# Attention pieces in DRAM as three rows to a channel, and another order of the work in a step

## The reference

```python
xn = layer_norm(x, norm_w, norm_b)                 # layer 0, 16 heads of 16 channels
q, k = xn @ q_w + q_b, xn @ k_w + k_b
att = softmax(einsum('bnhl,bmhl->bnmh', q, k) + (1 - mask) * -1e6, axis=2)
y = einsum('bnmh,bmhl->bnhl', att, (xn @ v_w + v_b) * mask)
scale, shift = split(silu(emb) @ emb_w + emb_b)
x = x + silu(layer_norm(y, sb_w, sb_b) * (1 + scale) + shift) @ out_w + out_b

xn = layer_norm(x, ln_w, ln_b)                     # layer 1, 8 heads of 32 channels
q = softmax(xn @ Wq + bq, over the head's channels)
k = softmax(xn @ Wk + bk + (1 - mask) * -1e6, over the tokens)
y = q @ (k^T @ ((xn @ Wv + bv) * mask))            # per head
x = x + silu(layer_norm(y) * (1 + scale) + shift) @ W_out + b_out
```

## Time and profile before

| | us |
|---|---|
| median of 3 runs (723.3 to 726.71) | 725.44 |
| the profiled execution | 723.0 |
| its span | 721.2 |
| PE busy in it | 579.2 |
| DVE busy | 441.6 |
| ACT busy | 351.3 |
| POOL busy | 65.9 |

### The profile page before, as it was taken

The page is one execution under the profiler, slowest core; times in us unless marked ns, Lnnn a source line. Parts: engine busy times, 40 slices in busy tenths (PEclk is TensorE's granted clock), DMA queues, the critical chain, the costliest instruction groups (busy, mean ns, idle before and its releaser), DMA issues.

```text
span 721.2 us, 7870 instructions
## 1 busy us (share of the span) xinstructions
PE 579.2 (80%) x2938; PEld 264.8 (37%) x2938; DVE 441.6 (61%) x891; ACT 351.3 (49%) x408; POOL 65.9 (9%) x85
## 2 busy tenths in 40 slices
PE   2608830899989988999998899999897999984875
PEld 1203510323334332434433333445333443333574
DVE  5134540457766896778788588777954788304443
ACT  0310200555556667565666656565545756671431
POOL 1021040000000003010001012000050101000300
PEclk9955855699999997999999799999966999997897
DMA  6143384003341000211102000000000000000001
GB/s 177 53 117 123 119 243 138 21 1 109 108 145 70 18 24 1 69 41 29 47 22 69 12 13 23 1 24 30 24 0 24 30 30 1 2 0 1 0 1 59
DMA packets 19494, 36.40 MB, mean 50 GB/s; under 512 B 3528, under 2 KB 10400, under 8 KB 19424
## 3 DMA queue, kind: packets, MB, share of 16 engines
q1 hardware_dynamic: 19264, 35.85, 16.7%
q10 hardware_dynamic: 192, 0.05, 0.0%
HBM read 20.76 MB, written 14.96 MB: 50 GB/s over the span
## 4 chain that ended last, share of the span: by engine, by line
PE 52%; DVE 17%; DMA 13%; ACT 6%; issue 4%; SPq 4%; ACTq 1%; POOL 0%; POOLq 0%; DVEq 0%
PE bank L849 13%; DMA stack_rows<-late 11%; DVE halfmax L972 10%; PE sT L830 9%; PE bank L738 8%; PE bank L717 8%; SPq L430 3%; PE bank L790 2%; PE sT L717 2%; PE bank L752 2%; DVE stats L903 2%; ACT prob L678 2%; DMA qs<-crows 2%; ACT hT L617 2%; PE bank L759 1%
## 5 line engine op out<-in xcount | busy, mean ns | idle before, releaser
L972 DVE TENSOR_REDUCE halfmax<-bank 128x1 f32<-128x512 f32 x512 | 325.3, 684 | 151.0 <-PE bank L738 149.5
L678 ACT ACTIVATE prob<-sT 128x1024 f32<-128x1024 f32 x256 | 257.4, 1023 | 185.2 <-PE sT L830 184.8
L738 PE MATMUL bank<-ks,qs 50*128 50x512 f32 x512 | 159.1, 455 | 42.7 <-DMA qs<-stack_rows 21.3
L830 PE MATMUL sT<-qs,ks 52*128 52x512 f32 x512 | 132.2, 507 | 45.4 <-DMA qs<-crows 34.5
L849 PE MATMUL bank<-prob,vp 128*17 128x512 f32 x1024 | 143.3, 633 | 4.2 <-ACT prob L678 4.2
L830 PEld LDWEIGHTS sT<-qs,ks 52*128 52x128 f32 x512 | 50.6, 192 | 178.6 <-issue 98.9
L738 PEld LDWEIGHTS bank<-ks,qs 50*128 50x128 f32 x512 | 73.0, 200 | 92.6 <-DVE halfmax L972 63.9
L534 POOL TENSOR_TENSOR rstd<-var,neghalf 128x4 f32<-128x4 f32 x14 | 14.2, 1015 | 591.8 <-DVE var L913 591.8
L717 PE MATMUL bank<-w,hT 128*128 128x256 f32 x144 | 39.1, 409 | 0.5
L849 PEld LDWEIGHTS bank<-prob,vp 128*17 128x17 f32 x1024 | 17.2, 96 | 43.9 <-issue 32.4
L717 PEld LDWEIGHTS bank<-w,hT 128*128 128x128 f32 x144 | 26.8, 202 | 9.0 <-DVE halfmax L972 3.5
(11 more groups left out here) (130 smaller groups left out, 461.0 us busy)
## 6 DMA issues: line engine op xcount, KB each, us to landing
stack_rows<-late SPq DMA_DIRECT2D x32, 256.0 KB
ks<-stack_rows SPq DMA_DIRECT2D x16, 400.0 KB
qs<-stack_rows SPq DMA_DIRECT2D x32, 192.0 KB, 3.4
stack_rows<-late SPq DMA_DIRECT2D x8, 512.0 KB
out_x<-xs SPq DMA_DIRECT2D x4, 512.0 KB, 3.0
xs<-in_x SPq DMA_DIRECT2D x4, 256.0 KB, 3.9
xs<-in_x SPq DMA_DIRECT2D x2, 512.0 KB, 6.5
late<-in_L_cond_emb_w SPq DMA_DIRECT2D x1, 1024.0 KB, 11.2
```

The source lines that it names most:

```text
L678: act.activation(prob[:, c % 2, 2 * u:2 * u + 2, :].rearrange("p j n -> p (j n)"), sT[u][:, :], ACT.Exp).then_inc(exp_done, 1)
L738: last = pe.matmul(o, qs[rows, s % SLOTS, c, t * P:(t + 1) * P], ks[rows, hg, c, half * HALF:(half + 1) * HALF], start=True, stop=True)
L830: last = pe.matmul(sT[u][:, two * HALF:(two + 1) * HALF], ks[rows, hg, u, c * P:(c + 1) * P], qs[rows, s % SLOTS, u, :], start=True, stop= ...
L972: dve.tensor_reduce(halfmax[:, s % 2, r, half:half + 1], o, axis=AX.X, op=ALU.max, negate=True).then_inc(u.done, 1)
```

## The change

It has four parts.

1. `stack_rows` becomes [group, 128 channels, 3 pieces, tokens]. A store writes 64 channels times two pieces, and 64 channels times one piece, for keys and for queries (four transfers instead of five). A load reads "(channel piece)" as 48 rows. The mask no longer goes through `stack_rows`: for batch 0 it is written into all of `ks` once, for batch 1 in two small transfers with every load of keys.
2. The rows of ones are filled from a longer source (1024 elements in `prob` instead of 128 in `ones`), so in fewer pieces. The 17 small loads go from ScalarE's queue to SyncE's, ahead of `store_parts(0)`. Store and keys of group 3, the embedding weights and `load_max(0)` stand in this order ahead of the other weights.
3. A step becomes: maxima 0, scores 0, scores 1, maxima 1, values of the step before, all small work of the step. ScalarE takes both exponentials, then the small work. The vector engine takes maxima 0, a middle part (low parts of "qk", half of the statistics), maxima 1, and the rest.
4. "y" and the layer norms that depend on it come one spot later, and the other items move with them: steps without any small work become 44 (37 before), steps with two items 24 (17).

```diff
         mask_rows = nc.dram_tensor("mask_rows", [B, PARTS, T], F32, kind="Internal").ap()
-        stack_rows = nc.dram_tensor("stack_rows", [G, 2 * GH, ROW_MAX, T], F32, kind="Internal").ap()
+        stack_rows = nc.dram_tensor("stack_rows", [G, P, PIECES, T], F32, kind="Internal").ap()
...
         for s in range(SUBS - 1):
-            at["y", s] = 2 * NT * (s + 1) + 1
+            at["y", s] = 2 * NT * (s + 1) + 2
...
-        spots = [(k, p) for k in range(STEPS + 2) for p in range(2)]
-        pe_at, act_at, dve_at = ({spot: [] for spot in spots} for _ in range(3))
-        begins = {key: (i // 2, i % 2) for key, i in at.items()}
-        for key, spot in begins.items():
-            assert spot[0] < STEPS
-            pe_at[spot].append(key)
+        pe_at, act_at, dve_mid, dve_at = ({k: [] for k in range(STEPS + 2)} for _ in range(4))
+        begins = {key: i // 2 for key, i in sorted(at.items(), key=lambda item: item[1])}
+        for key, k in begins.items():
+            assert k < STEPS
+            pe_at[k].append(key)
             if key[0] == "qk":
-                act_at[spot].append(key)
-                dve_at[later(spot)].append(key)
+                act_at[k].append(key)
+                dve_mid[k + 1].append(key)
             elif key[0] in ON_ACT:
-                act_at[spot].append(key)
+                act_at[k].append(key)
             else:
-                dve_at[spot].append(key)
...
             for i in range(QT):
-                dve_at[k, i // 2].append(("stats", kind, b, h, i))
-            dve_at[k + 1, 0].append(("aggr", kind, b, h))
+                (dve_mid if i < 2 else dve_at)[k].append(("stats", kind, b, h, i))
+            dve_mid[k + 1].append(("aggr", kind, b, h))
...
+        def dve_step(k):
+            if k >= STEPS:
+                return dve_mid[k] + dve_at[k]
+            return maxima(k, 0) + dve_mid[k] + maxima(k, 1) + dve_at[k]
...
-            sp.wait_ge(ones_ready, 1)
-            one = ones[0:PARTS, :].bitcast(F32).unsqueeze(1)
+            sp.wait_ge(one_ready, 1)
+            one = prob[0:PARTS, 0, 0:2, :].rearrange("r j n -> r (j n)").unsqueeze(1)
             for two in range(2):
                 rows = slice(two * TILE + ROW_MASK, two * TILE + ROW_MAX)
-                sp.dma_start(qs[rows, :, :, :].rearrange("r s c (a x) -> r (s c a) x", x=P).bitcast(F32), one.to_broadcast([PARTS, SLOTS * 2 * QT, P])).then_inc(rows_in, 16)
+                sp.dma_start(qs[rows, :, :, :].rearrange("r s c x -> r s (c x)").bitcast(F32), one.to_broadcast([PARTS, SLOTS, T])).then_inc(rows_in, 16)
                 rows = slice(two * TILE + ROW_MAX, two * TILE + ROWS)
-                sp.dma_start(ks[rows, :, :, :].rearrange("r s c (a x) -> r (s c a) x", x=P).bitcast(F32), one.to_broadcast([PARTS, HG * 2 * NT, P])).then_inc(rows_in, 16)
-
+                sp.dma_start(ks[rows, :, :, :].rearrange("r g c x -> r (g c) x").bitcast(F32), one.to_broadcast([PARTS, HG * 2, T])).then_inc(rows_in, 16)
             sp.wait_ge(mask_out, 16 * B)
-            for b in range(B):
-                sp.dma_start(stack_rows[b * HG:(b + 1) * HG, GH:2 * GH, ROW_MASK:ROW_MAX, :].rearrange("g x r n -> g x (r n)"),
-                             mask_rows[b].rearrange("r n -> (r n)").unsqueeze(0).unsqueeze(0).to_broadcast([HG, GH, PARTS * T])).then_inc(fill_in, 16)
+            for two in range(2):
+                rows = slice(two * TILE + ROW_MASK, two * TILE + ROW_MAX)
+                sp.dma_start(ks[rows, :, :, :].rearrange("r g c x -> r (g c) x").bitcast(F32), mask_rows[0].unsqueeze(1).to_broadcast([PARTS, HG * 2, T])).then_inc(rows_in, 16)
+            for at_row in (0, 32):
+                for i, src in enumerate((v_b, bq, bv)):
+                    sp.dma_start(braw[at_row:at_row + 1, i, :], src.rearrange("(o d) -> o d", o=1)).then_inc(braw_in, 16)
+            for name, src, n in (("sb_w", sb_norm_w, KC), ("sb_b", sb_norm_b, KC),
+                                 ("emb_b0", emb_b, 2 * KC), ("ln_w", ln_w, KC), ("ln_b", ln_b, KC), ("bk", bk, KC),
+                                 ("ln2_w", ln2_w, KC), ("ln2_b", ln2_b, KC), ("emb_b1", b_emb, 2 * KC),
+                                 ("cond", cond.rearrange("b e -> (b e)"), B * EC), ("mask1", mask1.rearrange("b t o -> (b t o)"), B * NT)):
+                loads(sp, name, src, n, vecs2, NV0, vec2_in)
 
             def store_parts(g):
 
                 last = unit["qk", g // HG, g % HG, NH - 1]
                 sp.wait_ge(last.done, last.done_at)
-                for xs_of, r, piece in ((slice(0, 2 * GH), 0, 0), (slice(0, GH), 1, 0), (slice(GH, 2 * GH), 2, 0), (slice(0, GH), 2, 1), (slice(GH, 2 * GH), 1, 1)):
-                    sp.dma_start(stack_rows[g, xs_of, r * DH0:(r + 1) * DH0, :], parts[xs_of.start * DH0:xs_of.stop * DH0, g % 2, piece, :]).then_inc(parts_out[g % 2], 16)
+                for side, both, single in ((1, 0, 2), (0, 1, 0)):
+                    rows = slice(side * GC, (side + 1) * GC)
+                    sp.dma_start(stack_rows[g, rows, both:both + 2, :], parts[rows, g % 2, :, :]).then_inc(parts_out[g % 2], 16)
+                    sp.dma_start(stack_rows[g, rows, single, :], parts[rows, g % 2, 0, :]).then_inc(parts_out[g % 2], 16)
 
             def load_keys(g):
                 if g >= HG:
                     sp.wait_ge(sT_ready, 2 * NT * (g + 1))
-                sp.wait_ge(parts_out[g % 2], 16 * 5 * (g // 2 + 1))
+                sp.wait_ge(parts_out[g % 2], 16 * 4 * (g // 2 + 1))
                 for two in range(2):
-                    sp.dma_start(ks[two * TILE:two * TILE + ROW_MAX, g % HG, :, :].bitcast(F32),
-                                 stack_rows[g, GH + 2 * two:GH + 2 * two + 2, :, :].rearrange("c r n -> r c n")).then_inc(k_in[g % HG], 16)
+                    src = stack_rows[g, GC + two * GC // 2:GC + (two + 1) * GC // 2, :, :].rearrange("(c p) r n -> (p r) c n", c=2)
+                    sp.dma_start(ks[two * TILE:two * TILE + ROW_MASK, g % HG, :, :].bitcast(F32), src).then_inc(k_in[g % HG], 16)
+                    if g >= HG:
+                        sp.dma_start(ks[two * TILE + ROW_MASK:two * TILE + ROW_MAX, g % HG, :, :].bitcast(F32),
+                                     mask_rows[g // HG].unsqueeze(1).to_broadcast([PARTS, 2, T])).then_inc(k_in[g % HG], 16)
 
             def load_queries(s):
                 b, n, hg, g = group(s)
                 if s >= SLOTS:
                     sp.wait_ge(sT_ready, 2 * NT * (s - SLOTS + 1))
                 for two in range(2):
-                    sp.dma_start(qs[two * TILE:two * TILE + ROW_MASK, s % SLOTS, :, :].bitcast(F32),
-                                 stack_rows[g, 2 * two:2 * two + 2, 0:ROW_MASK, n * HALF:(n + 1) * HALF].rearrange("c r n -> r c n")).then_inc(q_in[s % SLOTS], 16)
+                    src = stack_rows[g, two * GC // 2:(two + 1) * GC // 2, :, n * HALF:(n + 1) * HALF].rearrange("(c p) r n -> (p r) c n", c=2)
+                    sp.dma_start(qs[two * TILE:two * TILE + ROW_MASK, s % SLOTS, :, :].bitcast(F32), src).then_inc(q_in[s % SLOTS], 16)
...
             store_parts(2)
             load_keys(2)
             load_queries(2)
-            sp.dma_start(wo0[:, :, :], out_w.rearrange("(k p) c -> p k c", p=P)).then_inc(wo_in, 16)
+            store_parts(3)
+            load_keys(3)
+            for i, src in enumerate((emb_w, W_emb)):
+                sp.dma_start(embw[:, i], src.rearrange("(e p) c -> p e c", p=P)).then_inc(embw_in, 16)
+            load_max(0)
             for i, src in enumerate((out_b, b_out)):
                 sp.dma_start(bias_rows[:, i, :], src.partition_broadcast(P)).then_inc(row_in, 16)
-            for i, src in enumerate((emb_w, W_emb)):
-                sp.dma_start(embw[:, i], src.rearrange("(e p) c -> p e c", p=P)).then_inc(embw_in, 16)
-            store_parts(3)
-            load_keys(3)
+            sp.dma_start(wo0[:, :, :], out_w.rearrange("(k p) c -> p k c", p=P)).then_inc(wo_in, 16)
             for i, src in enumerate((Wq, Wk, Wv, W_out)):
                 sp.dma_start(w1[:, i], src.rearrange("(k p) c -> p k c", p=P)).then_inc(w1_in, 16)
...
+            pool.memset(prob[0:PARTS, 0, 0:2, :], 1.0).then_inc(one_ready, 1)
             pool.wait_ge(ident_ready, 1)
+            pool.wait_ge(one_ready, 1)
...
             act.dma_start(m16[:, :], mask0.rearrange("b (t p) -> (b t) p", p=P)).then_inc(m16_in, 16)
-            rows("norm_w", norm_w, KC, True)
-            rows("norm_b", norm_b, KC, True)
+            rows("norm_w", norm_w, KC)
+            rows("norm_b", norm_b, KC)
             for side, src in enumerate((q_b, k_b)):
                 act.dma_start(vecs[COL["qk_b"]:COL["qk_b"] + HG, side * GC:(side + 1) * GC],
                               src.rearrange("(g c) -> g c", c=GC)).then_inc(vec_in, 16)
-            rows("mask0", mask0.rearrange("b t -> (b t)"), B * NT, True)
+            rows("mask0", mask0.rearrange("b t -> (b t)"), B * NT)
             for h in range(NH):
```

(33 more changed lines are left out.)

## The result

The changed kernel takes 674.79 us (median of 4 runs, 673.9 to 676.24) beside 724.37 us of the kernel before on the same chip (4 runs, 720.7 to 726.71): a ratio of 0.932, 95% interval 0.928 to 0.937, or 49.6 us less. 668 us were forecast, with 643 to 690 as the range. Nearly all of it lies ahead of the main loop. First scores start at 85.6 us (128.8 before); from there to the start of the last values it is 513.0 us (519.8 before); the rest is 73.9 us, and 72.6 before (598.6 to 672.5, 648.6 to 721.2).

What follows compares the result with a forecast made beforehand. It took the slow transfers of queries and keys to DRAM ahead of the loop as the bound, with the loop near TensorE's limit. 723.0 - 54.8 - 2 = 666, as a median about 668 us; range 643 to 690.

Steps and rivals of the forecast that it cites:

- Part 1: Ahead of the loop, store 0 in its new shape lands 5.7 us behind its last issue, instead of 11.87 us.
- t0: The time at which store 0 begins: 28.34 us in the kernel before, forecast 21.1 us.
- Part 2: Start of store 0: with the 17 small loads moved to SyncE it begins at 21.1 us, -7.2 us.
- Part 3: From t0 to the loop: first scores at 74 us instead of 128.78, -54.8 us, t0's 7.2 among them.
- Part 4: Order within a loop step: empty steps 0.33 us shorter, many filled steps 0.3 to 0.65 longer; loop -2 us in all.
- A: Rival, main loop: waits for banks are absorbed, the loop gains 27 us instead of 2, 641 us; chance 0.17.
- B: Rival, main loop: about 75 filled steps pay 0.5 us or more, Silu stalls a microsecond each, 690 us; chance 0.14.
- D: Rival, main loop: the run of four costs more than the lead-in gives, 0.7 us a step, 750 us; chance 0.03.
- C: Rival, stores ahead of the loop: they don't gain what they should (173 GB/s or few engines), 677 us; chance 0.08.

## Why the prediction was right, point by point

**Direction and mechanism** were right: the slow stores in a row ahead of the loop were the bound, and the stores' shape was the cause. A store with four heads outermost ran at 0.25 of the engines, with 64 channels at 0.93. The rule in the Trainium skill, DMA: Bandwidth & Descriptors, "Why a DMA increments its semaphore by 16 and not by 1", gives four and sixteen engines for them, and the trace agrees. The 3.6 us that the prediction worked out by it for a store was too short against 5.65. It takes each engine to keep its rate. By that, 101 GB/s at a share of 0.25 would be some 376 at 0.93, and 225 were measured; why isn't shown.

**Part 1, a store:** 5.7 us and t0+8 were forecast. In the chain's count, from the start of the last issue, it took 5.65. But the prediction added the 5.7 to the end of the issues. It landed at t0+8.8: 4.4 us behind that end, and the four issues took 4.3 us instead of 2.3. Misses of 1.3 and 2 us nearly cancel there, which is luck.

**Part 2, t0,** failed. Forecast 21.1 us with bounds of 19 and 25, measured 27.78. I had seen the bias rows as what could be later and mis-sized when they land: 24.2 instead of 17.5 us. SyncE was through with the ones at 13.4 us, not 10.5; the issues of the mask rows ran to 16.5; and the landing took 5.8 us behind the last issue. The -7.2 us was therefore -0.6. With the bias rows first it was -6.6.

**Part 3, t0 to the loop:** forecast 52.5 us, measured 57.9. Its terms: first maximum at t0+14.7, measured t0+18.5, as keys and queries needed 8.9 us instead of 5.7 from the first issue; the maxima stage 34.3, measured 32.6 (46.31 to 78.92), within the bound named for an earlier rise of the granted clock, whose mean in the stage went from 0.70 to 0.85 (no run shows the clock's own part); the row's issues and landing 3.4, measured 6.3 (4.9 of it behind the issues, 2 forecast), for the weights that I had landing by t0+48: they were issued only from 74.0 us (t0+46), since the stores and loads ahead of them had run late one after the other (store 3 landed at t0+45, not t0+38).

The misses differ in kind. The row of maxima was priced from its row alone, with nothing for what lies ahead of it in the engines' queues, as the kernel with the embedding weights behind shows. The loads of keys and queries were priced near the rate of weights (1.15 MB in 3.3 to 4 us), and alone they move 153 to 217 GB/s.

**Part 4, the steps:**

| step | before | forecast | measured |
|---|---|---|---|
| empty | 2.93 | 2.6 | 2.69 |
| output projection, keys | 4.23 | 4.83 | 4.79, 4.84 |
| v, values | 4.47 | 4.77 | 4.85 |
| qk | 4.7 | 5.1 | 5.20 |
| y1 | 3.52 | 3.97 | 3.95 |

The forecast column is the old time plus the prediction's difference. The wait of the fourth maximum for a bank was the right mechanism: the step with the output projection shows it (252.88), and putting values ahead took 0.55 us off that step. The waits of the changed kernel have it too (who waited for whom, us in all, times, longest); the same row of the kernel before says 63.9 us:

```profile
PEld bank L740 <- DVE halfmax L972: 105.9, 176, 2.4
```

The sum in this row is no price, though: in the kernel with values ahead it is 125.3 us, and that loop is 10 us shorter. It counts idle time of the weight load, also where TensorE is busy.

Two kinds of steps came out better than forecast. Those with a row of maxima transposed take 2.91 us (3.5 to 3.7 before, 3.3 forecast), and those with eight transposes of the normalised x, for which nothing was counted, 3.71 (4.12 before). Yet the step order alone made the loop no shorter (521.6 us against 519.8), near the +3 us to which the prediction's terms for it add up. So other steps took the surplus back, and I haven't traced which.

The loop as a whole got 6.8 us shorter in this profile where 2 were forecast; with 3 us between two profiles of one kernel that is no clear difference. With the transfers alone it was 2.6 and 5.6 us shorter, so what there is comes with the transfers. The last ten steps went at about 2.2 us each, 2.05 forecast.

**The sum:** the start gave 43 us instead of 55, the loop 7 instead of 2. The second miss hides part of the first, and at 5 us it is little more than the 3 us by which two profiles differ. So far as it brought the time nearer to 668, that is luck.

The rivals: A (the loop gains 27 us) needed steps without the wait for banks; it is what the kernel with values ahead does, in part (502.9 us against 519.8). B and D didn't come. C's 677 us lies nearer the measured time than the forecast's 668, but its premise failed, as store 0 ran at a share of 0.93 and 225 GB/s. One part of it did come: the row of maxima waited behind store 3 and the weights. The times alone can't tell the forecast from C, the share can. A's 641 and B's 690 us leave out the 2 us that the forecast adds for the median; with them they are 643 and 692.

## What to carry to other kernels

Look at the DMA share while one transfer is alone: 0.25 of the engines with a queue of dependent transfers behind it was worth 43 us of 724, and one dimension in the tensor's layout sets it. Before small loads are moved to another queue, find who waits for the last of them: moved behind the mask rows they gained nothing, put first 6 us. Fewer switches of mode are no gain if they put all users of three banks in one run; let the work that needs no bank stand between them, which took 10.6 us off.

## What the hardware showed that I had not expected

A store of four heads with a gap between them and one of 4 times 16 channels without a gap look alike in the code; the first ran at a DMA share of 0.25, the second at 0.85, with 384 packets of 4 bytes more. Reading the rows back from DRAM keeps the engines busy (1.01) at 153 to 217 GB/s with nothing beside it, half of what weights get. And the issue of a 512 KB store on SyncE takes 0.53 us when the queue is empty and 1.86 us as the third in a row.
